# Gated recurrence of an eight-stage kernel: from a step per pair of groups with barriers to one unrolled program with four pipeline places

## The reference

```
q = silu(x @ Wq); v = x @ Wv
log_f = log_sigmoid(x @ Wk + delta); k = -expm1(log_f)
# 2 heads of 64; per token:
S = S * exp(g_t)[..., None] + k_t[..., None] * v_t[..., None, :]
o_t = einsum('bhk,bhkv->bhv', q_t, S)
...
o = o * sigmoid(x @ G1 @ G2)
og = og * rsqrt(mean(og * og, axis=-1) + EPS)     # per head
out = (og * norm_w) @ Wo                          # added to x
```

## Time and profile before

| what | us |
|---|---|
| median of three runs (6939.4 to 6947.73) | 6940.21 |
| the profiled execution, its own time | 6945.1 |
| its span, first to last instruction | 6943.3 |
| the stage, from the first DVE instruction of its layer norm to the end of its last add | 304.2 |
| one step of its steady part | 35.7 to 35.9 |

### The profile page before, as it was taken

The page is one execution under the profiler, slowest core; times in us unless marked ns, Lnnn a source line. Parts: engine busy times, 40 slices in busy tenths (PEclk is TensorE's granted clock), DMA queues, the critical chain, the costliest instruction groups (busy, mean ns, idle before and its releaser), DMA issues. The chain is left out here.

```text
span 6943.3 us, 128995 instructions
## 1 busy us (share of the span) xinstructions
PE 6121.0 (88%) x50945; PEld 3485.2 (50%) x50945; DVE 4359.7 (63%) x7548; ACT 3527.2 (51%) x5768; POOL 2189.2 (32%) x1461
## 2 busy tenths in 40 slices
PE   7999987999776666999657999999999999999998
PEld 4666664444432222666433555555555555555554
DVE  3444433444347777332447888888887888888885
ACT  2434333665434333444334665666666666666664
POOL 0000000222113334000004555555555555555553
PEclk9999987999868888999768999999999999999998
DMA  1000000222200000000001111111111111111111
GB/s 52 1 1 1 1 1 19 49 48 48 59 5 0 0 0 0 1 0 0 1 13 35 34 40 42 32 40 42 36 33 43 37 32 48 34 32 47 36 40 25
DMA packets 183550, 174.87 MB, mean 25 GB/s; under 512 B 24021, under 2 KB 174070, under 8 KB 182774
## 3 DMA queue, kind: packets, MB, share of 16 engines
q1 hardware_dynamic: 182998, 167.18, 10.1%
HBM read 30.79 MB, written 2.10 MB: 5 GB/s over the span
## 5 line engine op out<-in xcount | busy, mean ns | idle before, releaser
L2280 POOL TENSOR_TENSOR local_ssum<-local_sq 128x512 f32<-128x512 f32 x384 | 697.7, 1817 | 2298.1 <-ACT local_sq L2068 2297.7
L2288 POOL TENSOR_TENSOR local_rot<-local_rot,local_inv_all 128x512 f32<-128x512 f32 x768 | 957.6, 1279 | 90.3 <-DMA local_inv_all<-local_inv 89.9
L1889 PE MATMUL banks<-local_y,local_Wqkv 128*128 128x512 f32 x1536 | 823.9, 618 | 63.8 <-ACT local_sq L2068 61.0
L861 POOL TENSOR_TENSOR cosine_summed<-cosine_probs 128x512 f32<-128x512 f32 x128 | 174.6, 1364 | 1679.8 <-ACT cosine_probs L750 1679.8
L2090 ACT ACTIVATE local_probs<-local_probs,local_npeak 128x1152 f32<-128x1152 f32 x384 | 482.7, 1257 | 354.0 <-DVE local_probs L2194 354.0
L2194 DVE TENSOR_TENSOR local_probs<-banks,band 128x576 f32<-128x576 f32 x768 | 546.0, 752 | 182.8 <-PE banks L1924 177.4
L2174 DVE TENSOR_TENSOR local_rot<-banks,local_rotary_scaled 128x512 f32<-128x512 f32 x768 | 525.3, 684 | 193.3 <-PE banks L1889 187.6
L2068 ACT ACTIVATE local_sq<-banks 128x512 f32<-128x512 f32 x768 | 459.4, 598 | 247.4 <-DVE local_sin L2175 240.6
L2181 DVE TENSOR_TENSOR local_rot<-local_rot,local_sin 128x1024 f32<-128x1024 f32 x384 | 506.9, 1320 | 41.1 <-DVE local_sin L2175 1.4
L1924 PEld LDWEIGHTS banks<-local_rot 32*128 32x128 f32 x12288 | 415.1, 185 | 224.8 <-issue 200.6
L2084 ACT COPY local_v<-banks 128x512 f32<-128x512 f32 x384 | 224.8, 586 | 595.4 <-PE banks L1902 594.9
(11 more groups left out here) (401 smaller groups left out, 11057.1 us busy)
## 6 DMA issues: line engine op xcount, KB each, us to landing
local_inv_all<-local_inv SPq DMA_DIRECT2D x768, 128.0 KB, 2.7
cosine_inv_all<-cosine_inv SPq DMA_DIRECT2D x256, 128.0 KB, 2.7
local_Wqkv<-in_L_ffn_Wqkv_quads SPq DMA_DIRECT2D x36, 256.0 KB, 2.9
local_Wo<-in_L_ffn_Wo_quads SPq DMA_DIRECT2D x6, 512.0 KB, 4.1
experts_w_W<-in_L_ffn_W SPq DMA_DIRECT2D x1, 2048.0 KB
out<-x SPq DMA_DIRECT2D x8, 256.0 KB, 2.3
local_W<-in_L_ffn_W SPq DMA_DIRECT2D x12, 170.5 KB, 2.3
cosine_w_Wqkv<-in_L_attn_w_kv SPq DMA_DIRECT2D x1, 1024.0 KB
```

What stands on the lines that cost most here:

```text
L1889: pe.matmul(seqs(banks[:, QK_BANK, :]), Wqkv[:, at:at + P], y_group(g), start=True, stop=True).then_inc(qk_projected, 1)
L2280: pool.tensor_tensor(ssum[:, n % 2, m, :], sq[:, 0, :], sq[:, 1, :], ALU.add).then_inc(square_summed, 1)
L2288: pool.tensor_tensor(a, a, twice(inv_all[:, n % 2, m, of_seq(s)]), ALU.mult).then_inc(united, 1)
```

## The change

`gated_recurrence` no longer uses `pipeline`, `LayerNorm`, a loop or barriers between steps. It is one block; each engine runs i from -1 to 9 and does in iteration i parts of four groups: the layer norm of group i+1 (`ahead`), the making of group i (`m`), the work of group i-1 (`g`), and the gated norm and way out of group i-2 (`e`). Semaphores count up over the whole stage. The turned input `xnT` has two buffers; the layer norm's turn shares bank 7 with the way out, and `turn_out` waits for `xn_ready`. The gate (L1759 now) stays with the work; the square, reduction, root and scaling behind it go to the next iteration, in between the making's parts. `way_out` is split into `turn_out` and `project_out`. Silu now comes ahead of the two gate sigmoids. The block that waited for the weights and the unused `ndelta` are gone. Each instruction's shape is as before, and the stage issues as many matmuls. Cut to its core:

```diff
-        ln = LayerNorm(nc, ctx, consts, banks[:, 0, :], "hgrn_ln")
-        ndelta = sb("ndelta", [P, 1])
+        xn, xnT = sb("xn", [P, GT, D]), sb("xnT", [P, 2, GN])
...
+                def turn_x(m):
+                    pe.wait_ge(normed, GT * (m + 1))
+                    if m >= 3:
+                        pe.wait_ge(added, m - 2)
...
+                def turn_out(g):
+                    pe.wait_ge(o_normed, g + 1)
+                    pe.wait_ge(xn_ready, min(g + 3, GROUPS))
...
+                for i in range(-1, GROUPS + 2):
+                    m, g, e, ahead = within(i), within(i - 1), within(i - 2), within(i + 1)
+                    if m is not None:
+                        project(m)
+                    if g is not None:
+                        attend(g)
+                        turn_keys(g)
+                    if m is not None:
+                        project_values(m)
+                    if e is not None:
+                        turn_out(e)
+                    if g is not None:
+                        outer(g)
+                    if m is not None:
+                        project_gates(m)
+                    if e is not None:
+                        project_out(e)
+                    if g is not None:
+                        outputs(g)
+                    if ahead is not None:
+                        turn_x(ahead)
...
+                def sigmoids(m):
+                    act.activation(k[:, m % 2, :], z[:], ACT.Sigmoid, scale=-1.0).then_inc(k_sigmoid, 1)
+                    act.wait_ge(q_projected, m + 1)
+                    act.activation(q[:, m % 2, :], banks[:, Q_BANK, :], ACT.Silu).then_inc(q_silu, 1)
+                    for n in range(2):
+                        act.wait_ge(gates, 2 * m + n + 1)
+                        act.activation(half(sgate[:, m % 2], n), half_bank(n), ACT.Sigmoid).then_inc(gate_ready, 1)
+                    act.preload_act_table_set(EXP_LN)
...
+                    if e is not None:
+                        square(e)
+                    if m is not None:
+                        softplus(m)
+                    if e is not None:
+                        invert_norm(e)
+                    if g is not None:
+                        copy_keys(g)
+                    if m is not None:
+                        growths(m)
+                    if e is not None:
+                        take_out(e)
+                    if ahead is not None:
+                        root(ahead)
+                    if m is not None:
+                        sigmoids(m)
+                    if ahead is not None:
+                        copy_x(ahead)
...
+                    if ahead is not None:
+                        measure(ahead)
+                    if m is not None:
+                        take_projections(m)
+                    if e is not None:
+                        mean_square(e)
+                    if g is not None:
+                        mask(g)
+                    if m is not None:
+                        decays(m)
+                        take_values(m)
+                    if e is not None:
+                        normalize_out(e)
+                    if g is not None:
+                        states(g)
+                    if ahead is not None:
+                        normalize_x(ahead)
+                    if e is not None:
+                        add_out(e)
+                    if m is not None:
+                        decayed(m)
+                    if g is not None:
+                        gate(g)
+        restart(nc, [*norms, *made, *worked, *ended])
```

More of the change, by code:

```diff
@@ L1459, in gated_recurrence @@
         oT = sb("oT", [P, GN])
[L1460 to L1470, removed]
+        norms = (stats_done, moments_done, var_done, log_done, rstd_done, normed, turned, xn_ready) = signals(
+            nc, ctx, "hgrn_stats hgrn_moments hgrn_var hgrn_log hgrn_rstd hgrn_normed hgrn_turned hgrn_xn_ready")
@@ L1700, in gated_recurrence, with measure @@
-        pipeline(nc, step)
+                def measure(m):
+                    for t in range(GT):
+                        dve.bn_stats(stats[:, t, :], tiles(m)[:, t, :]).then_inc(stats_done, 1)
+                    dve.wait_ge(stats_done, GT * (m + 1))
+                    for t in range(GT):
+                        dve.bn_aggr(moments[:, t, :], stats[:, t, :]).then_inc(moments_done, 1)
+                    dve.wait_ge(moments_done, GT * (m + 1))
+                    if m:
+                        dve.wait_ge(log_done, m)
+                    dve.tensor_scalar(var[:], moments[:, :, 1], LN_EPS, None, ALU.add).then_inc(var_done, 1)
@@ new lines, in take_values, with decays @@
+                def take_values(m):
+                    for n in range(2):
+                        dve.wait_ge(v_ready, 2 * m + n + 1)
+                        if m >= 2:
+                            dve.wait_ge(o_ready, m - 1)
+                        dve.tensor_copy(half(vals[:, m % 2], n), half_bank(n)).then_inc(v_copied, 1)
+                def decays(m):
+                    dve.wait_ge(mag_log, m + 1)
+                    dve.scalar_tensor_tensor(logf[:], z[:], 0.0, mag[:], ALU.min, ALU.subtract).then_inc(logf_ready, 1)
+                    dve.wait_ge(logf_ready, m + 1)
+                    if m:
+                        dve.wait_ge(enG_ready, m)
+                    dve.tensor_tensor_scan(G[:], consts["inside"], logf[:], 0.0, ALU.mult, ALU.add).then_inc(G_ready, 1)
@@ new lines, in normalize_out, with add_out @@
+                def normalize_out(g):
+                    dve.wait_ge(rms_ready, g + 1)
+                    oh = o[:].rearrange("p c (h d) -> p (c h) d", d=HW)
+                    dve.tensor_tensor(oh, oh, spread(rms[:], HW), ALU.mult).then_inc(o_normed, 1)
+                def add_out(g):
+                    dve.wait_ge(out_ready, g + 1)
+                    dve.tensor_tensor(tiles(g), tiles(g), banks[:, END_BANK, :].rearrange("p (t d) -> p t d", d=D), ALU.add).then_inc(added, 1)
+                for i in range(-1, GROUPS + 2):
+                    m, g, e, ahead = within(i), within(i - 1), within(i - 2), within(i + 1)
+                    if ahead is not None:
[21 more added lines that the diff above has]
+                        gate(g)
```

391 lines of the change are left out of this document (193 added, 198 removed).

## The result

The changed kernel takes 6891.36 us (median of four runs, 6887.70 to 6894.51), the kernel before 6943.73 beside it (four runs, 6939.4 to 6947.73). The ratio is 0.9926, with a 95% interval from 0.991 to 0.9941: faster by 52 us. The forecast was 100 us, 6840, with a range of 6826 to 6866, so the time lies outside it. It lies where rival 1 put it, 6890. The profiled execution took 6894.5 us.

The account below looks back on a forecast made before the run. The stage was taken as bound by waits, not an engine. 41 + 6 x 23.0 + 15.5 + 10.2 = 204.7 us against 304.2, with 0.5 for the head: 100 us off 6940.2, so 6840, range 6826 to 6866.

Parts of the forecast that it names:

- rival 1: Half clock isn't left again within an iteration: period 31.4 us, 50 us more, 6890; chance 0.08.
- the ring: Period is VectorE's string from gate to scaling, 11.3, plus TensorE's from `turn_out` to `outputs`, 10.8: 22.1 us at full clock.
- a z that is late by more than 1 us: Sign of a wrong prediction: VectorE waits over 1 us for z or the mask, the ring then running through x's turn.
- Start and drain: Stage start to first gate 41 us, bounds 38 to 44; from last gate to the end 10.2 us.
- the pause: TensorE waits 2 to 3 us once a period for the scaling, ahead of `turn_out`.
- the term of the clock: Clock falls in some periods as TensorE's string begins, slowing the turn and `outer`: 0.9 us on the mean, period 23.0.
- The last period: Stretch up to the last gate, with no making beside it: 15.5 us, from 16.3 in the kernel before.
- The sign that was named for this step: The prediction is wrong if the clock reads 0.50 for more than 4 us of a period.
- rival 2: Clock at half throughout, TensorE the bound with about 35 us a period: 6928; chance 0.02.
- rival 3: ScalarE's four table loads each have a further pause of 1.4 us: period 26 to 27, 6868; chance 0.03.
- rival 4: Slower than before: engines wait for fetched code of the loop body laid out in full, 6972 at 12 us; chance 0.02.
- rival 5: Better than the bounds: VectorE overlaps more and the start is shorter, below 6826; chance 0.07.

Follow-up runs that it names:

- experiment 1: Kernel after plus two extra 512-column matmuls ahead of `turn_out`, in TensorE's wait for the scaling: 6844.88 us, ratio to before 0.9857.
- experiment 9: experiment 8 with three extra 512-column matmuls ahead of `turn_out` instead of two: 6855.98 us, one run.
- experiment 10: experiment 1 with an extra VectorE reduction behind the add to x, outside VectorE's string: 6844.33 us, one run.
- experiment 5: Kernel after with `outer` moved ahead of `turn_out` and the Wq projection moved right ahead of `turn_out`, nothing added: 6829.94 us, ratio to before 0.9834.
- experiment 4: Kernel after plus two extra 512-column matmuls ahead of `outputs`, the pause left as it is: 6889.72 us, one run.
- experiment 3: Kernel after with `outer` moved ahead of `turn_out`, nothing added: 6861.4 us, ratio 0.9881.
- experiment 7: Kernel after with only the Wq projection moved right ahead of `turn_out`, `outer` staying behind it: 6891.84 us, one run.
- experiment 2: Kernel after plus eight extra small matmuls (64x128) ahead of `turn_out`, in the pause: 6856.93 us, one run.
- experiment 8: experiment 1 with a second VectorE reduction of 1.2 us ahead of the mean square's own, inside VectorE's string: 6878.76 us, one run.

## Why the prediction was wrong

**Right: the ring.** It was worked out as 11.3 + 10.8 = 22.1 us at the full clock; experiment 1 measured 10.98 + 10.6 = 21.60. Experiments 9 and 10 show that VectorE's string is part of it, and experiment 5 shows the same of TensorE's. The forecast had also named a z that is late by more than 1 us as a sign of being wrong. It is late by 1.18 us, but with the clock, not with the ring: experiment 1 reaches 21.60 us. Start and drain were right within 1.4 us and 0.1 us. The head gave 0.8 us (1.35 from the experts' last addition to the first statistics, 2.19 before), for which 0.5 stood. What else differs between the profiled executions lies outside the stage, in unchanged code: 1.8 us less in all.

**Right: the pause.** 2 to 3 us before `turn_out` were expected, and 2.66 are there.

**Wrong: the term of the clock.** "I take 0.9 as a mean, between 0 and 1.7" is the step that failed. Measured in the period shown it is 29.93 - 21.60 = 8.3 us, and 11.3 in that of 32.93. Of the step's two halves, the first (in some periods the clock falls as the string begins) was too mild: it fell in every one. The second, that only the turn and `outer` run slow "until it is back", was wrong in kind: it doesn't come back in TensorE's string. The 8.3 us lie there (17.0 - 10.6 = 6.4) and, through the Wk projection at the half clock and the late z and low, in VectorE's string (12.9 - 11.0 = 1.9). The last period, 21.25 us instead of 15.5, has the same fault in part: it is at 0.50 throughout, and 18.19 with wide work in it (experiment 4), though still 21.08 in experiment 1, where only its first part is at the full clock. And it has one more: the 15.5 were taken from a length in which the turn and Wo of another group were not queued, 3.2 us at the half clock. The sign that was named for this step, a clock at 0.50 for more than 4 us of a period, is there five times over: some 20 us, from 3508 to 3528. The range couldn't catch it either. Its upper end took a period of 24.7, and the terms given for it (22.1 + 1.7) make 23.8.

**Why rival 1 got only 0.08.** Its price was right: period 31.4 against a mean of 30.8 measured, time 6890 against 6891. That it was so close is partly luck: TensorE's string took 17.0 us in the period shown, not 20.1, VectorE's 12.9, not 11.3, and the six periods' 3.4 us too many stand against 5.8 too few in the last. The argument against it was that in before the clock had come back some 5 us after a longer idle time. The trace of before shows that in seven steps of eight, in small matmuls too:

```profile
3496.80:3498.30 1.50, 1.50 (x16) 0.50 0.00 0
3498.30:3499.80 1.50, 1.50 (x8) 0.50 0.00 0
3499.80:3501.30 1.50, 1.26 (x10) 0.85 0.00 0
```

But rows 5 were the eighth. In the first working step the same work began at 3347.8, `outer` still took 3.78 us at 3352.68, and the clock was back only at 3360, behind two projections of 512 columns; and the sentence of rival 2, that a busy TensorE "in every row here brought the full clock", was not true of those rows. I used rows 5 for a price and didn't read them as a case of rival 1. In the kernel after the second kind is the rule: all five returns of the clock behind a fall in a period came in the wide projections or, once, in the matmuls right behind them.

**Refuted: rivals 2 to 5.** The clock isn't at half throughout (0.60 to 0.67). Instruction traffic is 392 packets instead of 387, and a period at the full clock has no length left for it. The time wasn't better than the bounds. For rival 3, the row of the load at 3507.48 ends at 3508.76 and its activation starts at 3508.78: no drain is seen, and experiment 1 reaches 21.60 us with the same four loads. The Trainium skill ("ScalarE: Activation LUTs", section "What ACT_TABLE_LOAD costs") states some 1.38 us of drain on top of a load of 1.28; the measurement disagrees here.

**Open.** The runs don't settle what exactly the clock follows. Experiments 1, 3, 5 and 7 show that the pause's length and the wide work near it act together, but as odds and not as a rule: behind 0.68 us it fell four times in six (experiment 3), behind 0.91 three times in six (2), behind 1.65 four times in four (8), and behind 0.75 with two wide matmuls ahead never in experiment 1 and once in experiment 10, with the same work on TensorE. They don't tell why, nor why experiment 5 loses it in its sixth period, or why the periods of after alternate between 29.9 and some 32.7. The returns in small matmuls in seven steps of before, and in experiments 2 and 5, stand beside 16 us of such matmuls in after without one, and no run isolates the difference. Each experiment's periods are those of one profiled execution.

## What to carry to other kernels

Where a change removes barriers, work out the ring (each engine's queue between two hand-overs) from the orders of the two queues, and then price the clock separately, stretch by stretch, with "it stays at half until the next wide projections" as a full case. If TensorE's queue keeps one wait of some us in a period, first move independent work into it until little of the wait is left, and put the widest of it right ahead of what is left; here two such moves, with nothing added, were worth more than the whole restructuring had brought (61 us against 52). And when a row of the trace is used for a price, ask also of which rival it is an instance.

## What was not expected of the hardware

- TensorE, busy for 1.50 of every 1.50 us shown, stayed at a granted clock of 0.50 from 3508 to 3523.7 in matmuls of 64 and 128 columns.
- Adding two 512-column matmuls per iteration into a wait of 2.66 us made the kernel 46 us faster (6891.4 to 6844.9).
- The clock could fall while the engine was busy: behind a wait of 0.68 us at 3451 it read 1.00 up to 3454 and then 0.57 and 0.50, with TensorE busy throughout.
- 1.2 us more on VectorE cost 34 us of the kernel (6844.9 to 6878.8, experiments 1 and 8; one run of the latter). At the full clock it costs 0.9 us a period (experiment 9), so most of the 34 came through the clock.
- The same work on TensorE around the same pause of 0.75 us kept the clock six times in experiment 1 and lost it once in six in experiment 10.
